# Adding the fourth key tile to the running sums on GpSimd, and one piece less in the products with ones

## The reference

```
x = x + tanh(g_xattn) * attention(layernorm(x), ctx, ctx, causal mask, 16 heads of 32)
x = x + tanh(g_ffn) * channel_mix(layernorm(x))
attention:   softmax(q k^T / sqrt(32), causal) v, then the output projection
channel_mix: sigmoid(xr Wr) * (relu(xk Wk)^2 Wv), xr and xk mixed with the token before
```

## Time and profile before

| | us |
|---|---|
| median of 3 runs | 2025.04 (2024.98 to 2026.63) |
| the profiled execution, its own time | 2026.49 |
| its span | 2024.8 |
| PE busy | 1928.9 (95%) |
| DVE busy | 1374.1 (68%) |
| POOL busy | 1293.4 (64%) |
| ACT busy | 969.1 (48%) |

### The profile page before, as it was taken

The page is one execution under the profiler, slowest core; times in us unless marked ns, Lnnn a source line. Parts: engine busy times, 40 slices in busy tenths (PEclk is TensorE's granted clock), DMA queues, the critical chain, the costliest instruction groups (busy, mean ns, idle before and its releaser), DMA issues. The chain is left out here.

```text
span 2024.8 us, 36616 instructions
## 1 busy us (share of the span) xinstructions
PE 1928.9 (95%) x11648; PEld 1500.2 (74%) x11648; DVE 1374.1 (68%) x3534; ACT 969.1 (48%) x1870; POOL 1293.4 (64%) x1829
## 2 busy tenths in 40 slices
PE   4899999999999999999999999994599999999999
PEld 3677777777777777777777777762488888888887
DVE  3767677777777777777777777764466675656663
ACT  4555555555555555555555555544243434334341
POOL 4566666666666666666666666656277787777771
PEclk9999999999999999999999999996799999999999
DMA  5544554455544455544465454551222223231311
GB/s 183 109 113 120 134 144 118 118 122 132 145 119 120 121 129 149 120 120 121 125 152 122 114 126 121 132 154 51 76 71 98 88 78 109 67 117 65 103 63 63
DMA packets 128665, 229.31 MB, mean 113 GB/s; under 512 B 18656, under 2 KB 20704, under 8 KB 127616
## 3 DMA queue, kind: packets, MB, share of 16 engines
q1 hardware_dynamic: 128512, 227.43, 42.3%
HBM read 92.06 MB, written 33.59 MB: 62 GB/s over the span
## 5 line engine op out<-in xcount | busy, mean ns | idle before, releaser
L701 DVE CUSTOM_DVE_ANT_0 score_ps<-score_ps,causal 128x128 f32<-128x128 f32 (+3 forms) x1024 | 487.5, 504 | 291.1 <-PE score_ps L855 290.1
L533 ACT ACTIVATE probs<-prob_ps 128x512 f32<-128x512 f32 (+1 forms) x768 | 394.3, 528 | 405.0 <-PE prob_ps L879 202.3
L855 PE MATMUL score_ps<-k_stack,q_stack 97*128 97x128 f32 (+3 forms) x1024 | 319.8, 354 | 6.5 <-DVE least L701 2.9
L879 PE MATMUL prob_ps<-q_stack,k_stack 100*128 100x512 f32 (+3 forms) x1024 | 285.6, 320 | 12.6 <-DMA q_stack<-max_rows 7.4
L385 POOL TENSOR_SCALAR_AFFINE_SELECT probs<-probs 128x256 f32<-128x256 f32 x256 | 106.2, 415 | 259.9 <-ACT probs L533 259.8
L396 POOL TENSOR_TENSOR prob_sum<-probs 128x384 f32<-128x384 f32 x256 | 262.7, 1026 | 0.0
L855 PEld LDWEIGHTS score_ps<-k_stack,q_stack 97*128 97x128 f32 x1024 | 189.7, 191 | 53.4 <-issue 13.3
L879 PEld LDWEIGHTS prob_ps<-q_stack,k_stack 100*128 100x128 f32 x1024 | 194.0, 193 | 33.6 <-DMA q_stack<-max_rows 8.9
L399 POOL TENSOR_TENSOR prob_sum<-prob_sum,probs 128x256 f32<-128x256 f32 x256 | 188.5, 736 | 36.7
L389 POOL TENSOR_SCALAR_AFFINE_SELECT probs<-probs 128x256 f32<-128x256 f32 x256 | 104.5, 408 | 159.0 <-ACT probs L533 158.8
L896 PE MATMUL value_ps<-probs,v 128*32 128x512 f32 (+3 forms) x2048 | 154.0, 442 | 13.2 <-POOL prob_sum L399 13.1
(11 more groups left out here) (145 smaller groups left out, 4910.5 us busy)
## 6 DMA issues: line engine op xcount, KB each, us to landing
k_stack<-staged_k_high SPq DMA_DIRECT2D x256, 128.0 KB
q_stack<-staged_q_high SPq DMA_DIRECT2D x256, 128.0 KB, 3.1
tiles<-in_x SPq DMA_DIRECT2D x16, 1024.0 KB, 5.6
k_stack<-staged_k_low SPq DMA_DIRECT2D x128, 128.0 KB
q_stack<-staged_q_low SPq DMA_DIRECT2D x128, 128.0 KB, 3.1
x_io<-in_x SPq DMA_DIRECT2D x16, 1024.0 KB, 7.8
x<-x_io SPq DMA_DIRECT2D x64, 256.0 KB, 2.9
wk_low_room<-x SPq DMA_DIRECT2D x16, 1024.0 KB, 5.5
```

Of the source, the lines that this page charges most:

```text
L533: nc.scalar.activation(probs[:, u % RING, lo:hi], prob_ps[(3 * u + c) % 2][:, 0:hi - lo], ACT.Exp, scale=SCALE).then_inc(exp_done, 1)
L701: nc.vector.tensor_tensor_reduce(out=here, in0=here, in1=causal[:, LATE - P * t:S], scale=-1.0, scalar=3e38, op0=ALU.add, op1=ALU.min, acc ...
L855: last = nc.tensor.matmul(here[:, at:at + P * (t + 1)], q_stack[n][0:MASK_ROW + 1, j, P * t:P * t + P], k_stack[n][0:MASK_ROW + 1, j, 0:P ...
L879: last = nc.tensor.matmul(here[:, at:at + width], k_stack[n][0:ROWS, j, P * k:P * k + P], q_stack[n][0:ROWS, j, P * k:S], start=True, stop ...
```

## The change

sum_probs gets a third addition, of tile 3's 128 columns to the last 128 columns of prob_sum, behind a wait for the second. summed counts three steps for each head, so values(G) waits for 3 * HG * (G + 1). The four products of line 907 for each group are gone, and the four of line 904 open and close their accumulation themselves.

```
                 pool.wait_ge(masked, 2 * u + 2)
-                pool.wait_ge(summed, 2 * u + 1)
+                pool.wait_ge(summed, 3 * u + 1)
                 nc.gpsimd.tensor_tensor(total[:, P:LATE], total[:, P:LATE], here[:, PT_AT[2]:PT_AT[2] + 2 * P], ALU.add
+                                        ).then_inc(summed, 1)
+                pool.wait_ge(summed, 3 * u + 2)
+                nc.gpsimd.tensor_tensor(total[:, 2 * P:LATE], total[:, 2 * P:LATE], here[:, PT_AT[3]:PT_AT[3] + P], ALU.add
                                         ).then_inc(summed, 1)
...
-                pe.wait_ge(summed, 2 * HG * (G + 1))
+                pe.wait_ge(summed, 3 * HG * (G + 1))
...
                 for j in range(HG):
-                    nc.tensor.matmul(sum_ps[DH * j:DH * j + DH, P:S], ones[:], prob_sum[:, (HG * G + j) % RING, :],
-                                     start=True, stop=False, skip_group_check=True)
-                for j in range(HG):
-                    last = nc.tensor.matmul(sum_ps[DH * j:DH * j + DH, LATE:S], ones[:],
-                                            probs[:, (HG * G + j) % RING, PT_AT[3]:PT_AT[3] + P],
-                                            start=False, stop=True, skip_group_check=True)
+                    last = nc.tensor.matmul(sum_ps[DH * j:DH * j + DH, P:S], ones[:], prob_sum[:, (HG * G + j) % RING, :],
+                                            start=True, stop=True, skip_group_check=True)
                 last.then_inc(values_done, 1)
```

## The result

| | before | after |
|---|---|---|
| median of 6 runs, us | 2024.45 (2022.22 to 2026.63) | 2033.03 (2028.87 to 2033.92) |
| ratio after / before | | 1.0039, 95% interval 1.0027 to 1.0052 |
| profiled execution, us | 2026.49 | 2028.87 |

The change made the kernel slower by 0.4%, 8 to 9 us, where 9 us less was forecast. The profiled execution of after is its fastest run.

The account below looks back on a forecast made before the run. The prediction took TensorE to bound the attention phase, with POOL some 29 us free per sequence. Its terms, -13.8 + 3.1 + 1.8 = -8.9 us, gave 2016.1 us from a median of 2025.04, range 2010.5 to 2024.0.

Parts of the forecast that it names:

- The products, -13.8 us: On TensorE, 64 sets of four removed products save 13.8 us; 0.11 us of switching per set stays.
- The length of an addition, 0.46 us: POOL's new two-input addition of 128 columns was to take 0.46 us, from the means of wider ones.
- The gap ahead of it, 0.15 us: POOL's wait before each new addition was taken as 0.15 us, not 0.08, making a head 0.61 us longer.
- values(4b) waits 0.22 us for POOL in 14 sequences, +3.1 us: Three heads' additions need 1.83 us where 1.61 are free, so TensorE waits there: 3.1 us in all.
- values(0) has 78.90 - 76.84 = 2.06 us, enough for 1.83: At the first values group, POOL's room of 2.06 us was to cover three heads' delay of 1.83 us.
- Behind POOL's small steps ACT waits: ACT's layernorm of the next sequence starts 0.6 us later, set at no cost; 8 us if cover is gone.
- L711 meets the first in place of the second: Bias additions shift 1.2 us; DVE's subtraction for the maxima meets the other one, ending within 0.1 us of before.
- 0.05 after the L711: TensorE's turn of the maxima starts 0.05 us after DVE's subtraction at 562.98: a spot without cover in each sequence.
- The end, +1.8 us: At values(63), where POOL is the path, three additions cost 1.8 us, at least 1.2 if one is hidden.
- Rival 2: Contention: the new addition holds DVE's subtraction L711 by 0.46 us at uncovered spots, costing 6.9 to 20.7 us; chance 0.12.
- Rival 1: Half the products' gain is lost to TensorE's waits at maxima turns and exponentials: 2023.0 us, no change; chance 0.13.
- Rivals 3 and 4: POOL's chain outgrows its room, 2028.7 us, chance 0.08; line 904's products slow when also closing accumulation, 2029.9 us, chance 0.02.

Follow-up runs that it names:

- b_remove: Kernel before without the four products for key tile 3, no POOL addition in their place: 2010.0 us, ratio 0.9931.
- a_bias4: Changed kernel with the residual's second pair of bias additions in slot 4 in place of slot 3: 2014.4 us, 0.9947 of the kernel before.
- b_shift: Kernel before, all products kept, plus a one-input POOL mask of 256 columns into a spare tile for each head: 2045.5 us, ratio 1.0104.
- b_add_two: Kernel before, all products kept, plus the third POOL addition into a spare tile for two heads of sixteen: 2038.8 us, ratio 1.0072.
- a_after: The changed kernel run again unaltered, as base for the runs beside it: 2032.8 us, 1.0035 of the kernel before.

## Why the prediction was wrong, point by point

- **The products, -13.8 us.** Right: 14.4 measured alone (b_remove). The 0.11 us of switching stayed: behind the last set the scores start 0.75 us after its start (563.75 to 564.50).
- **The length of an addition, 0.46 us.** Right: 0.473 in the mean, 0.46 in most.
- **The gap ahead of it, 0.15 us.** Mis-sized: the wrong choice between the two ends: 577.51 to 577.59 is 0.08. A head became longer by 0.52 us (from the second L396 to the third in slots 6 to 8: 3.12 against 2.60).
- **values(4b) waits 0.22 us for POOL in 14 sequences, +3.1 us.** Wrong: it does not wait. POOL's chain from the first mask (566.35 us) to the end of the last sum became 1.62 us longer, what the small gap would give (3 x 0.54); TensorE came 0.38 later, so that 0.43 lie between them. The delay had reached TensorE by another way first.
- **"values(0) has 78.90 - 76.84 = 2.06 us, enough for 1.83."** Wrong: it waits 1.14 us (b_remove: 0.34 there, with POOL as before). The 2.06 were read in an execution in which TensorE was granted the lower clock, 0.50, from 72.7 to 79.5 us, and so came late; in the profile after it is 1.00 there. Some 0.8 us, once.
- **"Behind POOL's small steps ACT waits ... I set that at nothing. If that cover is gone it is 0.6 us on 14 sequences, 8 us."** This step failed. ACT's idle time of the slot lay behind the place where it was needed: the application stood ahead of an exponential with which TensorE was just in time. 0.33 to 0.40 us in a sequence, 5 to 6 us.
- **"L711 meets the first in place of the second, and I take it that it ends within 0.1 us of where it did."** This is the step that turned the sign. It followed only the subtraction L711. The CAST in front of it (L709), of one input, is not in the prediction, and it is held in the same way: the CAST met the first addition, and L711 met the second again. The split ends 2.4 us after the CAST's start and not 1.3. Cost: 13 waits of 1.19 us in the trace of after, 1.07 more in each than before: 13.9 us. In the other two of the fifteen sequences the split came a little earlier and met one bias addition or none; the turn followed its product by 0.73 and 0.23 us.
- **"0.05 after the L711", no cover but no cost.** The turn had lost 0.29 us there already. a_bias4 gained it.
- **The end, +1.8 us.** Right in kind: 1.4 (14.6 against 13.2).
- **Rival 2 (contention, a loss of 6.9 to 20.7 us).** Nearest to what happened, at one of the spots it named. Its mechanism was another: it had the new addition hold L711 by its 0.46. b_shift shows that a new step which reads one input costs the same, and b_add_two that only the shift of the bias pair matters there. In the whole trace of after a held CAST or subtraction starts beside the new addition only twice (0.33 and 0.31 us).
- **Rival 1.** Refuted by b_remove.
- **Rivals 3 and 4.** Neither came: the additions took 0.47 us and values(4b) does not wait in those 14 sequences, and the scores start 0.75 us after the start of the set of L907, the time of the set and the switch before (0.65 + 0.11).
- **"If L711's and L732's mean times grow."** L711's grew little (0.600 to 0.619 us), the CAST's from 0.248 to 0.354, and L732's fell from 1.18 to 0.79. Nothing was gained there: TensorE waits for it once, 2.8 us before and 2.9 after.

The sum with the measured terms is -14.4 + 13.9 + 6 + 1.4 + 0.8 = +7.7 us; measured +8.6 by the medians, and +7.8 in a_after.

The Trainium skill's rule that the forecast weighed (GPSIMD Engine Reference, Specifications: GpSimd contends with VectorE's instructions in a two-port mode or with two SBUF inputs) has two halves; I used the second only. The CAST has one input in SBUF and took 1.20 us and not 0.17. That fits the first half if the CAST runs in a two-port mode, which no trace here shows.

## What to carry to other kernels

Before you delay an engine, write down every instruction of it that moves, and lay all of them beside what the other engine does at the moved times; here the harm came from two bias additions that the diff does not touch. Follow whole chains, the small instruction in front of the critical one too. Read cover from the starts of instructions and not from the list of waits, and set a delayed step at nothing only when its engine's idle time lies between it and the next thing that is waited for.

## What the runs showed of the hardware

- A DVE instruction of 0.17 us that starts beside a POOL instruction becomes as long as that has still to run. In the trace of after 153 of the 256 CASTs and subtractions of the split are longer than 0.18 us, and each of them ends 0.02 to 0.03 us after a POOL instruction: CASTs beside a mask, which has one input, take up to 0.38 us, subtractions beside an addition of 384 columns 0.94, and beside the bias additions of 512 columns 1.20. Two such DVE instructions in a row, beside two POOL additions in a row, were held by one each (1.20 + 1.18): what POOL did next began before DVE's next.
- The reverse holds as well: POOL's addition of 128 columns took 2.38 us and not 0.46 beside DVE's subtraction of 2048 columns, and that of 384 columns 3.07 and not 1.01.
- POOL's two-input additions take 0.46 us for 128 columns, 0.74 for 256, 1.01 for 384, 1.29 for 512.
- The profiled executions differ by up to 5 us already at values(4) (before 163.2, after 158.5, a_after 161.1 us), while a sequence of the changed kernel takes 84.54 us in one and 84.55 in the other. In the trace before TensorE's granted clock is 0.50, the level of 1.2 GHz, from 72.7 to 79.5 us and again from 106.8 to 110.2, the second time behind a wait of 1.76 us for a DMA; in the trace after it is 1.00 in both stretches, and that wait is absent. What decides it was not looked for. A margin that is read in such a stretch, like the 2.06 us at values(0), need not be there in the next execution.
